# A message path folded into the next weight matrix: root spread by four transposes, squares on ScalarE, and work passed between VectorE and GpSimd

## The chip, the cores and the metric

The kernel runs on one core of one Trainium2 chip. The metric is the device time of one execution in microseconds (us); the time of before is the median of three runs. TensorE is PE in the rows, VectorE is DVE, ScalarE is ACT, GpSimd is POOL, SyncE is SP.

## What is computed

One layer for a graph of 12,500 nodes with 256 channels: a graph part on gathered rows, a linear-attention mixer, and a mixture of four experts. Cut to what matters:

```python
xn = layernorm(x)
# graph part: one gathered row of dst per node, four heads of 64, weights from a softmax over heads
tmp = einsum('nh,nhd->nd', alpha[:n], xt[col[:n]])         # xt = xn @ weight
# mixer
Q, K = elu(xn @ Wq) + 1, elu(xn @ Wk) + 1
KV = einsum('nshd,nshv->nhdv', K, v)                        # one matrix per head, summed over all nodes
msg = (Q KV / (Q . sum K)) @ Wm
msg = layernorm(msg, g1, b1)
h   = relu(concat([xn, msg]) @ W1) @ W2
x1  = x + tmp (four times side by side) + xn + layernorm(h, g2, b2)
# experts, on layernorm(x1)
out = x1 + shared_mlp + the two best of four experts, weighted by a softmax of their gates
```

## The kernel before

Nodes are taken in 25 groups of 512 (four tiles of 128 rows; the last group has two tiles of 106 rows). Every product but a few small ones is done as three fp32r products: each operand is split into a high part, rounded to fp32r, and a low part, what is left (`split_mm`, L272 to L274). So each activation needs a `_hi` copy (ScalarE) and a `_lo` subtraction (VectorE or GpSimd) before TensorE can take it.

**Phase 1** (`phase1`, to about 250 us) runs over the groups and sums K, v and the tables of the graph part. In its last three groups `small_constants` and `second_parts` prepare the weights on VectorE, among them the high and low parts of W1, whose message half (rows 256 to 511) is scaled by `g1`.

**The seam** (`turn0`, `turn1` and the turn of `second=True`, 250 to 341 us) ends the sums, makes `kvT` and `G` (`g_hi`, `g_lo`: the per-head matrices times Wm), and fills the pipeline of the second phase.

**Phase 2** (`phase2(i, par)`) is a loop of turns, i = 3 to 24, then `last_turn` and `end_turn`. Three groups are in flight: group i (a: query, denominators, message), group i-1 (b: the hidden layer W1, W2, the residual `base`, the graph part `gnn`) and group i-2 (c: shared MLP, experts, gates, output). Every engine runs its own fixed program, written out by hand in the order of the code, and waits on semaphores (`wait_ge`) that others count up. Nothing reorders it.

The message path, which the change touches, goes so: `p2_m` makes rows of the message in PSUM (banks 6 and 7); VectorE takes mean and variance of each row (`bn_m`, `mv_m`); GpSimd makes `rs_m` = 1/sqrt(variance + eps) and `nm_m` (`rstd`); ScalarE writes the normalised rows `row_n` (`message_rows`); at the start of the next turn TensorE turns them (`transposes(row_n, ...)`, eight of 128x128) into PSUM banks 0 and 1; ScalarE and VectorE split that into `mT_hi` and `mT_lo`; TensorE multiplies them with the message half of W1 (`w1_part(1, ...)`), after 12 products of `w1_part(0, ...)` and 12 of `p2_q` that stand between.

The z path of the same turn goes: `row_z` (ScalarE), eight transposes, `z_hi` (ScalarE), `z_lo` (VectorE, L1507 in the loop), then the products of the shared MLP, the gates and the experts. `feature_low` (L1335) and `feature_high` (L1341) stand with an exponential between them (ScalarE, L983) for the query. `soft_chain_in` (L1373 to L1386), `compare` and `top_weights` make the gate rows (L1437). GpSimd does `h_lo` (twice a turn), `s1_lo` (shown as `s_lo`, L1841), the sum of `base` and `gnn` (L1865) and eight gathers by indirect DMA.

## Time and profile before

| | |
|---|---|
| time, median of three runs | 1325.66 us (1324.2 to 1329.84) |
| the profiled execution | 1322.97 us |
| its span, first to last instruction | 1321.1 us |
| TensorE busy | 1292.3 us |
| VectorE busy | 1105.4 us |
| ScalarE busy | 733.8 us |
| GpSimd busy | 770.7 us |
| mean granted TensorE clock | 0.997 of full |

The profiled execution is one of its own beside the three timed ones; its span leaves out what lies before the first and behind the last instruction. Busy time is the union of the instructions of an engine. The ends of matmuls are modelled, so two of them overlap in the rows, and the distance from start to start says what one costs.

### The profile page before, as it was taken

What the parts mean: (1) busy time and instruction counts of PE and PEld (TensorE: products, weight loads), DVE (VectorE), ACT (ScalarE), POOL (GpSimd) and SP (SyncE); (2) the same over time, 40 slices, a digit from 0 to 9 for tenths busy, and PEclk for the clock granted to TensorE, in tenths of its full rate; (3) what the DMA queues carried; (4) which work ended last, traced back from release to release, by engine and by line L of the source; (5) the groups of instructions that cost most, each with busy time, mean ns of one, the idle gap of its engine ahead of it and who ended that gap; (6) DMA issues with size and microseconds to landing.
All of it is one profiled execution on the core that took longest, in us unless ns stands there. A gap on an engine that the chain in (4) does not pass through costs nothing.

```text
span 1321.1 us, 26301 instructions
## 1 busy us (share of the span) xinstructions
PE 1292.3 (98%) x8812; PEld 1119.4 (85%) x8812; DVE 1105.4 (84%) x2597; ACT 733.8 (56%) x1332; POOL 770.7 (58%) x815
## 2 busy tenths in 40 slices
PE   6999999899999999999999999999999999999998
PEld 5999999876888888888888888888888888888876
DVE  6988777978888888888888888888888888888875
ACT  4555555345645655455645655555645655555654
POOL 5777777745546654655556564655555654655531
PEclk9999999899999999999999999999999999999999
DMA  6787766523212221222111221222111221212000
GB/s 206 245 283 253 251 226 223 165 61 73 65 42 60 77 75 29 76 60 80 50 54 56 80 73 32 76 60 80 44 60 56 80 72 32 76 60 71 26 17 23
DMA packets 65459, 123.23 MB, mean 93 GB/s; under 512 B 31725, under 2 KB 36176, under 8 KB 65422
## 3 DMA queue, kind: packets, MB, share of 16 engines
q1 hardware_dynamic: 57422, 109.25, 25.6%
q0 software_dynamic: 8000, 13.53, 4.8%
q8 instruction: 19, 0.31, 0.1%
q14 instruction: 18, 0.15, 0.0%
HBM read 70.41 MB, written 52.32 MB: 93 GB/s over the span
## 4 chain that ended last, share of the span: by engine, by line
PE 88%; DVE 4%; issue 3%; POOL 2%; DVEq 1%; POOLq 1%; ACT 1%; ACTq 0%
PE psum L272 26%; PE psum L273 25%; PE psum L274 25%; PE psum L484 5%; PE psum L676 3%; PE psum L729 1%; PE psum L667 1%; PE psum L566 1%; PE psum L739 1%; PE psum L559 1%; POOL h_lo L1841 1%; POOL ag L1837 0%; POOLq L1775 0%; POOL xg L1835 0%; DVE kf L1249 0%
## 5 line engine op out<-in xcount | busy, mean ns | idle before, releaser
L1841 POOL TENSOR_TENSOR h_lo<-relu,h_hi 128x1024 fp32r<-128x1024 f32 (+1 forms) x50 | 119.8, 2397 | 142.1 <-ACT h_hi L998 142.0
L272 PE MATMUL psum<-w_hi,h_hi 128*128 128x256 f32 x588 | 164.4, 280 | 1.6 <-POOL h_lo L1841 1.5
L273 PE MATMUL psum<-w_lo,h_hi 128*128 128x256 f32 x588 | 163.8, 278 | 0.0
L274 PE MATMUL psum<-w_hi,h_lo 128*128 128x256 f32 x588 | 163.7, 278 | 0.0
L1841 POOL TENSOR_TENSOR s_lo<-relu,s_hi 128x512 fp32r<-128x512 f32 (+1 forms) x45 | 82.5, 1834 | 95.8 <-ACT s_hi L1099 94.3
L272 PE MATMUL psum<-z_hi,w_hi 128*128 128x512 f32 (+1 forms) x300 | 121.6, 405 | 2.0 <-DVE z_lo L1611 1.1
L1835 POOL DMA_INDIRECT xg<-table_xt,idx x100 | 99.5, 995 | 34.9 <-issue 31.9
L272 PE MATMUL psum<-xT_hi,w_hi 128*128 128x512 f32 (+1 forms) x300 | 119.4, 398 | 0.1
L997 ACT ACTIVATE relu<-psum,h_bias 128x512 f32<-128x512 f32 (+1 forms) x100 | 67.8, 678 | 88.5 <-PE psum L274 88.4
L273 PE MATMUL psum<-xT_lo,w_hi 128*128 128x512 f32 (+1 forms) x300 | 116.9, 390 | 0.0
L274 PE MATMUL psum<-xT_hi,w_lo 128*128 128x512 f32 (+1 forms) x300 | 116.7, 389 | 0.0
L273 PE MATMUL psum<-z_lo,w_hi 128*128 128x512 f32 (+1 forms) x300 | 116.6, 389 | 0.0
L274 PE MATMUL psum<-z_hi,w_lo 128*128 128x512 f32 (+1 forms) x300 | 116.2, 387 | 0.0
L272 PEld LDWEIGHTS psum<-w_hi,h_hi 128*128 128x128 f32 x588 | 110.4, 188 | 3.5 <-POOL h_lo L1841 1.9
L1837 POOL DMA_INDIRECT ag<-table_al,idx x100 | 95.2, 952 | 30.5 <-issue 30.5
L274 PEld LDWEIGHTS psum<-w_hi,h_lo 128*128 128x128 f32 x588 | 111.4, 190 | 0.0
L273 PEld LDWEIGHTS psum<-w_lo,h_hi 128*128 128x128 f32 x588 | 110.5, 188 | 1.0
L915 ACT ACTIVATE row_n<-psum,nm_m,rs_m 128x256 f32<-128x256 f32 x98 | 47.4, 564 | 111.4 <-POOL nm_m L1778 111.4
L1470 DVE SCALAR_TENSOR_TENSOR base<-xb,rn,b_bc 128x256 f32<-128x256 f32 x98 | 91.7, 975 | 0.2 <-issue 0.2
L1009 ACT ACTIVATE e<-psum,e_bias 128x512 f32<-128x512 f32 (+1 forms) x100 | 67.3, 676 | 37.2 <-PE psum L274 37.1
L272 PE MATMUL psum<-mT_hi,w_hi 128*128 128x512 f32 (+1 forms) x200 | 80.1, 401 | 0.9 <-DVE mT_lo L1619 0.9
L1811 POOL TENSOR_TENSOR k_lo<-kf,k_hi 128x1024 fp32r<-128x1024 f32 x25 | 63.0, 2521 | 30.3 <-DVE k_hi L1253 30.3
(274 smaller groups left out, 4298.1 us busy)
## 6 DMA issues: line engine op xcount, KB each, us to landing
xb<-in_x SPq DMA_DIRECT2D x47, 448.0 KB, 3.5
xT_hi_table<-x1T_hi SPq DMA_DIRECT2D x25, 512.0 KB, 2.8
xT_lo_table<-x1T_lo SPq DMA_DIRECT2D x25, 512.0 KB, 3.6
xT_hi<-xT_hi_table SPq DMA_DIRECT2D x25, 512.0 KB, 3.8
xT_lo<-xT_lo_table SPq DMA_DIRECT2D x25, 512.0 KB, 4.7
table_xt<-xts SPq DMA_DIRECT2D x24, 455.0 KB, 3.0
out<-xmid SPq DMA_DIRECT2D x24, 448.0 KB
xb<-in_x SPq DMA_DIRECT2D x47, 64.0 KB, 3.6
```

Of the source, the lines that this page charges most:

```text
L272: pe.matmul(out, wh, xh, start=first, stop=False)
L273: pe.matmul(out, wh, xl, start=False, stop=False)
L274: return pe.matmul(out, wl, xh, start=False, stop=last)
L484: last = pe.transpose(psum[:, b + c, j * R:(j + 1) * R], src[:, j, c * P:(c + 1) * P], ident[0:R, 0:R])
L915: act.activation(out[:, j, :], src(j), ACT.Identity, bias=nm[which][:, j:j + 1], scale=rs[which][:, j:j + 1]).then_inc(S[done], 1)
L997: act.activation(out[:, 0:t * R], colT(b, t=t), ACT.Relu, bias=bias)
L1009: act.activation(e1[:, e, 0:t * R], colT(bank, t=t), ACT.Relu, bias=e1_bias[:, e:e + 1]).then_inc(S["e1_relu"], 1)
L1470: last = stt(base[:, j, :], xb[par][:, j, :], rn2[par][:, 0, j:j + 1], b2_bc[:], ALU.mult, ALU.add)
L1811: ptt(k_lo[par][:], kf[par][:], k_hi[par][:], ALU.subtract).then_inc(S["k_split"], 1)
L1835: pool.indirect_dma_start(xg[par][:, j, :], None, table_xt.ap(), bass.IndirectOffsetOnAxis(idx[par][:, 1, j:j + 1], 0)).then_inc(S[f"gath{ ...
L1837: pool.indirect_dma_start(ag[par][:, j, :], None, table_al.ap(), bass.IndirectOffsetOnAxis(idx[par][:, 0, j:j + 1], 0)).then_inc(S[f"gath{ ...
L1841: ptt(out, src, hi, ALU.subtract).then_inc(S[done], 1)
```

## The change

- **The message is no longer normalised in rows.** The mean is taken out by centring the rows of Wm (`wm`, in `small_constants`). `G` times diag(g1) times the message half of W1 is multiplied out once, in the seam (`gT`, then four fp32 products of 128x512 on TensorE, split by ScalarE and VectorE into `w_hi` and `w_lo`). What W1 is applied to is then the query over its denominator (`qm`, transposed already), times the root `rs_m` of each node.
- **The root** needs the mean square of the message rows only. `p2_m` stays; `message_squares` on ScalarE replaces `bn_m` on VectorE, `message_rstd` on GpSimd has two small operations instead of four. `spread_deviation` on TensorE spreads the root over the partitions: four transposes whose loaded operand is `rs[:, j:j+1]` read 128 times, into one bank, instead of the eight of `row_n`. `over_deviation` on VectorE multiplies `qm` by it. ScalarE then copies `mT_hi` from `qm`, and VectorE makes `mT_lo` (`message_low`).
- **Between VectorE, ScalarE and GpSimd**: `s1_lo` and the sum of `base` and `gnn` go from GpSimd to VectorE, behind the gate rows. The first of four heads of `gnn` goes to ScalarE (`first_head`). Two residual rows instead of one stand early in VectorE's turn. ScalarE's exponential of the query stands ahead of the first relu pair. GpSimd's gathers for the next group stand right behind the second `h_lo`.

```diff
+            def spread_deviation(i, b, t=T):
+
+                pe.wait_ge(S["rs_m"], i)
+                for j in range(t):
+                    last = pe.transpose(psum[:, b, j * R:(j + 1) * R], rs[LM][:, j:j + 1].broadcast_to([R, P]),
+                                        ident[0:R, 0:R])
+                last.then_inc(S["mt"], 1)
...
+            last.then_inc(S["g_mm"], 1)
+            for c in range(CK):
+                for q in range(CK):
+                    last = pe.matmul(psum[:, 0, c * C + q * P:c * C + (q + 1) * P], wm[:, q, c * P:(c + 1) * P],
+                                     kvT[:, q, :], start=True, stop=True)
+            last.then_inc(S["gt_mm"], 1)
...
-                transposes(row_n, MT2_BANK if second else 0, "mt", "m_norm", T * (i - 1))
+                spread_deviation(i, MT2_BANK if second else 0)
                 w1_part(0, 2, 6, xT_old)
                 w1_part(0, 3, 7, xT_old).then_inc(S["xT_free"], 1)
                 if second:
-                    pe.wait_ge(S["mT"], i)
+                    pe.wait_ge(S["qm"], i)
...
+                p2_den(1, 2)
+                pe.wait_ge(S["gt"], 1)
+                for q in range(CK):
+                    for c in range(CK):
+                        last = pe.matmul(psum[:, q, :], gT[:, c, q * P:(q + 1) * P], wslice(w_raw, "W1", 2 + c),
+                                         start=c == 0, stop=c == CK - 1)
+                    last.then_inc(S["gw_mm"], 1)
+                pe.nop().then_inc(S["p1_pe"], 1)
...
-                p2_den(1, 2)
-                transposes(row_n, 0, "mt", "m_norm", 0)
+                spread_deviation(1, 3)
                 w1_part(0, 2, 6, xT0)
                 w1_part(0, 3, 7, xT0).then_inc(S["xT_free"], 1)
+                pe.wait_ge(S["qm"], 1)
+                p2_expand(1, 2)
+                pe.wait_ge(S["gw_split"], 1)
                 pe.wait_ge(S["mT"], 1)
-                for o in range(2):
-                    w1_part(1, o, 4 + o, mT).then_inc(S["h_mm"], 1)
-                p2_expand(1, 2)
-                for o in range(2, 4):
+                for o in range(4):
                     w1_part(1, o, 4 + o, mT).then_inc(S["h_mm"], 1)
                 pe.wait_ge(S["h_relu"], 2)
...
+            def first_head(v, par):
+
+                act.wait_ge(S["gates"], v - 1)
+                act.wait_ge(S["base"], v)
+                act.wait_ge(S[f"y{par}"], 4 * dma16(v, par))
+                for j in range(T):
+                    last = act.activation(gnn[:, j, :], xg[par][:, j, 0:HEAD_CH], ACT.Identity,
+                                          bias=rn2[par][:, 1, j:j + 1], scale=soft_e[:, 1, j, 0:1])
+                last.then_inc(S["gnn0"], 1)
...
+                if not second:
+                    first_head(i - 1, 1 - par)
+                act.wait_ge(S["qm"], i)
+                act.activation(mT_hi[:], qm[:], ACT.Copy).then_inc(S["mT_hi"], 1)
...
                     z_rows()
+                    p2_exp(i)
                     act.wait_ge(S["e2_lo"], i - 2)
                     first_relu(0)
-                    p2_exp(i)
                     z_high()
...
+            def message_squares(i):
+
+                if due(i):
+                    act.wait_ge(S["rs_m"], i)
                 t = tiles(i)
-                normalize(row_n, lambda j: rowt(6, j, t), LM, "m_norm", t)
+                for pair in range(2):
+                    act.wait_ge(S["m_mm"], 2 * i + pair + 1)
+                    for j in pair_of(pair, t):
+                        last = act.activation(rowt(6, j, t), rowt(6, j, t), ACT.Square,
+                                              scale=1.0 / math.sqrt(C), accum_out=ssq[:, j:j + 1])
+                last.then_inc(S["ssq"], 1)
...
+                dve.reduce_sum(wm_nmean[:], wm[:], AXX)
...
+                for c in range(CK):
+                    ts(wm[:, c, :], wm[:, c, :], wm_nmean[:, c:c + 1], None, ALU.add)
...
-            dve.wait_ge(S["w_hi"], 3)
-            for c in range(CK):
-                stt(wslice(w_lo, "W1", 2 + c), wslice(w_raw, "W1", 2 + c), g1_col[:, c:c + 1],
-                    wslice(w_hi, "W1", 2 + c), ALU.mult, ALU.subtract)
...
+            def over_deviation(i, b, t=T):
+
+                now = slice(0, t * R)
+                dve.wait_ge(S["mt"], i)
+                tt(qm[:, :, now], qm[:, :, now], colT(b, t=t).unsqueeze(1).broadcast_to([P, CK, t * R]),
+                   ALU.mult).then_inc(S["qm"], 1)
+
+            def message_low(i, t=T):
+                now = slice(0, t * R)
+                dve.wait_ge(S["mT_hi"], i)
+                tt(mT_lo[:, :, now], qm[:, :, now], mT_hi[:, :, now], ALU.subtract).then_inc(S["mT"], 1)
+
             def phase2(i, par, a=True, b=True, c=True, more=True, second=False):
-                if b:
+                if b and second:
                     residual(i - 1, 1 - par, (0,))
                 if b and not second:
-                    dve.wait_ge(S["mT_hi"], i)
-                    tt(mT_lo[:], colT(0, 2), mT_hi[:], ALU.subtract).then_inc(S["mT"], 1)
-                if b and not second:
-                    graph_layer(i - 1, 1 - par)
-                if a and not second:
+                    over_deviation(i, 0)
...
+                    residual(i - 1, 1 - par, (0, 1))
+                    message_low(i)
+                    graph_layer(i - 1, 1 - par, (1,))
                     feature_low(i, Q_BANK)
+                    graph_layer(i - 1, 1 - par, (2, 3))
                     feature_high(i, Q_BANK)
...
+                if b and c and not second:
+                    dve.wait_ge(S["s1_relu"], 2 * (i - 1))
+                    tt(s1_lo[:], relu[2][:], s1_hi[:], ALU.subtract).then_inc(S["s1_lo"], 1)
+                    bv = base[:].rearrange("p j (h d) -> p j h d", h=HEADS)
+                    tt(bv, bv, gnn[:].unsqueeze(2).broadcast_to([R, T, HEADS, HEAD_CH]), ALU.add).then_inc(S["base"], 1)
...
-                if a:
-                    if due(i):
-                        dve.wait_ge(S["rs_m"], i)
-                    for pair in range(2):
-                        dve.wait_ge(S["m_mm"], 2 * i + pair + 1)
-                        stats(LM, pair_of(pair, t), lambda j: rowt(6, j, t))
-                    aggregate(LM, "mv_m")
...
+                over_deviation(1, 3)
+                dve.wait_ge(S["gw_hi"], 2)
+                tt(w1_message(w_lo), psum[:, 0:2, :], w1_message(w_hi), ALU.subtract).then_inc(S["gw_split"], 1)
+                message_low(1)
...
+            def message_rstd(count):
+
+                pool.wait_ge(S["ssq"], count)
+                if due(count - 1):
+                    pool.wait_ge(S["mt"], count - 1)
+                ptt(veps[LM][:], ssq[:], eps[:], ALU.add)
+                pool.drain()
+                ptt(rs[LM][:], veps[LM][:], neg_half[:], ALU.pow).then_inc(S["rs_m"], 1)
...
+                        if n == 1 and ahead:
+                            pool.wait_ge(S["gnn"], i)
+                            pool.wait_ge(S[f"idx{1 - par}"], 2 * dma16(i + 1, 1 - par))
                         if due(4 * (i - 1) + 2 * n + 2):
                             pool.wait_ge(S["h_relu"], 4 * (i - 1) + 2 * n + 2)
                         low(h_lo[:, 2 * n:2 * n + 2, :], relu[n][:], h_hi[:, 2 * n:2 * n + 2, :], "h_lo")
...
-                if c and not seam:
-                    if due(2 * (i - 1)):
-                        pool.wait_ge(S["s1_relu"], 2 * (i - 1))
-                    low(s1_lo[:], relu[2][:], s1_hi[:], "s1_lo")
-                if b:
-                    if due(i):
-                        pool.wait_ge(S["t"], i)
-                    if due(i):
-                        pool.wait_ge(S["gnn"], i)
-                    if ahead:
-                        pool.wait_ge(S[f"idx{1 - par}"], 2 * dma16(i + 1, 1 - par))
-                    if not seam:
-                        bv = base[:].rearrange("p j (h d) -> p j h d", h=HEADS)
-                        ptt(bv, bv, gnn[:].unsqueeze(2).broadcast_to([R, T, HEADS, HEAD_CH]),
-                            ALU.add).then_inc(S["base"], 1)
-                    if ahead:
-                        gathers(1 - par, (0, 1))
+                if ahead:
+                    gathers(1 - par, (0, 1))
```

TensorE, the start of a turn (`psum` is the output in all rows; above it the last output products of the turn before). Before:

```order
L273 MATMUL psum<-w_lo,h_hi 128x256
L274 MATMUL psum<-w_hi,h_lo 128x256
L484 MATMUL psum<-ident,row_n 128x128 x8
L272 MATMUL psum<-xT_hi,w_hi 128x512
L273 MATMUL psum<-xT_lo,w_hi 128x512
L274 MATMUL psum<-xT_hi,w_lo 128x512
```

and in the change:

```order
L281 MATMUL psum<-w_lo,h_hi 128x256
L282 MATMUL psum<-w_hi,h_lo 128x256
L503 MATMUL psum<-ident,rs_m 128x128 x4
L280 MATMUL psum<-xT_hi,w_hi 128x512
L281 MATMUL psum<-xT_lo,w_hi 128x512
L282 MATMUL psum<-xT_hi,w_lo 128x512
```

Eight transposes of `row_n` became four of `rs_m`; the products around them are the same.

VectorE, the start of the turn that follows the loop, of the same order as those in it. Before:

```order
L281 COMPARE_AND_BRANCH
L1470 SCALAR_TENSOR_TENSOR base<-xb,rn_0,b_bc 128x256
L1496 TENSOR_TENSOR mT_lo<-psum,mT_hi 128x1024
L1484 TENSOR_SCALAR gnn<-xg,soft_e,rn_0 128x64 x4
L1486 SCALAR_TENSOR_TENSOR gnn<-xg,soft_e,gnn 128x64 x12
L1335 TENSOR_SCALAR qf<-psum 128x1024
L1341 SCALAR_TENSOR_TENSOR qf<-psum,qf 128x1024
```

and in the change:

```order
L289 COMPARE_AND_BRANCH
L1545 TENSOR_TENSOR qm<-qm,psum 128x1024
L1518 SCALAR_TENSOR_TENSOR base<-xb,rn_0,b_bc 128x256 x2
L1551 TENSOR_TENSOR mT_lo<-qm,mT_hi 128x1024
L1536 SCALAR_TENSOR_TENSOR gnn<-xg,soft_e,gnn 128x64 x4
L1387 TENSOR_SCALAR qf<-psum 128x1024
L1536 SCALAR_TENSOR_TENSOR gnn<-xg,soft_e,gnn 128x64 x8
L1393 SCALAR_TENSOR_TENSOR qf<-psum,qf 128x1024
```

The product with the spread (`qm`) and a second residual row stand ahead of `mT_lo`, one head of `gnn` has left, and the other three stand around the low part of the query (`qf`, first row).

VectorE behind the gate rows of a turn in the loop, before and in the change:

```order
L1435 CAST scale_rows<-top_hi 128x4x4 x2
L1437 TENSOR_TENSOR scale_rows<-top_e,top_hi 128x4x4
L1527 REGISTER_ALU
L1211 BN_STATS bn_y<-psum 128x6 x2
L1537 REGISTER_ALU
L1538 TENSOR_TENSOR qf<-qf,psum 128x512
```

```order
L1483 CAST scale_rows<-top_hi 128x4x4 x2
L1485 TENSOR_TENSOR scale_rows<-top_e,top_hi 128x4x4
L1589 TENSOR_TENSOR s_lo<-relu,s_hi 128x1024
L1591 TENSOR_TENSOR base<-base,gnn 128x1024
L1594 ISA
L1260 BN_STATS bn_y<-psum 128x6 x2
L1604 REGISTER_ALU
L1605 TENSOR_TENSOR qm<-qf,psum 128x512
```

`s_lo` and the base sum stand now between the gate rows and the statistics of y.

## Rows read from the trace of the kernel before

**Rows 1.** The page, parts 1 and 2: busy time (share) and instructions; clock in 40 slices.
```profile
PE 1292.3 (98%) x8812; PEld 1119.4 (85%) x8812; DVE 1105.4 (84%) x2597; ACT 733.8 (56%) x1332; POOL 770.7 (58%) x815
...
PEclk9999999899999999999999999999999999999999
```

**Rows 2.** Table of stretches: length; busy of PE, PEld, DVE, ACT, POOL; clock; DMA.
```profile
256.00:262.00 6.00, 6.00 (x34) 4.95 (x31) 4.17 (x12) 0.00 (x0) 4.67 (x5) 0.58 0.33 55
640.00:682.50 42.50, 42.50 (x277) 35.72 (x276) 36.45 (x90) 24.09 (x43) 24.13 (x26) 1.00 0.22 62
```

**Rows 3.** TensorE's waits, 225 to 330 us: total, times, longest.
```profile
PE psum L633 <- DVE kx L1359: 1.8, 1, 1.8
PE psum L272 <- POOL k_lo L1811: 1.4, 1, 1.4
PE psum L559 <- DVE qf L1341: 1.0, 1, 1.0
PE psum L484 <- ACT row_z L915: 0.8, 1, 0.8
```

**Rows 4.** TensorE's waits, 1270 to 1300 us.
```profile
PE psum L272 <- DVE z_lo L1611: 1.1, 1, 1.1
PE psum L272 <- DVE mT_lo L1619: 0.9, 1, 0.9
```

**Rows 5.** TensorE in order of time (start, duration in us), and the tile row_n (ns).
```profile
341.52 1.04 PE L484 MATMUL psum<-ident,row_n 128*128 128x128 f32 x8
342.31 0.48 PE L272 MATMUL psum<-xT_hi,w_hi 128*128 128x512 f32 x1
...
1274.70 0.60 PE L484 MATMUL psum<-ident,row_n 128*128 128x128 f32 x4
1275.06 0.36 PE L272 MATMUL psum<-xT_hi,w_hi 128*128 128x256 f32 x1
...
L484 PE MATMUL psum<-ident,row_n x196: 271/272/330, 272.5 to 1275.0; 128*128 128x128 f32 x196
```

**Rows 6.** The turn that starts at 639.6 us, in order of time: PE, DVE, ACT.
```profile
645.79 0.39 PE L274 MATMUL psum<-xT_hi,w_lo 128*128 128x512 f32 x1
646.02 0.40 PE L272 MATMUL psum<-mT_hi,w_hi 128*128 128x512 f32 x1
...
652.42 0.39 PE L272 MATMUL psum<-z_hi,w_hi 128*128 128x512 f32 x1
...
639.81 1.22 DVE L1590 TENSOR_TENSOR xmid<-xmid,psum 128x1024 f32<-128x1024 f32 x1
...
650.99 1.21 DVE L1507 TENSOR_TENSOR z_lo<-psum,z_hi 128x1024 fp32r<-128x1024 f32 x1
...
648.77 1.05 ACT L983 ACTIVATE qf<-qf 128x1024 f32<-128x1024 f32 x1
649.86 1.03 ACT L1033 ACTIVATE z_hi<-psum 128x1024 fp32r<-128x1024 f32 x1
```

**Rows 7.** The same turn, DVE and POOL: small operations beside large ones.
```profile
658.73 1.84 DVE L1373 TENSOR_TENSOR soft<-ag,xg 128x16 f32<-128x16 f32 x1
...
660.73 2.19 DVE L1381 SCALAR_TENSOR_TENSOR soft<-soft 128x16 f32<-128x16 f32 x1
...
658.13 2.41 POOL L1841 TENSOR_TENSOR s_lo<-relu,s_hi 128x1024 fp32r<-128x1024 f32 x1
```

**Rows 8.** The seam in order of time: DVE and PE.
```profile
252.16 1.41 DVE L1354 SCALAR_TENSOR_TENSOR w_lo<-w_raw,g_col,w_hi 128x512 fp32r<-128x512 f32 x2
...
296.45 1.23 DVE L1735 TENSOR_TENSOR mT_lo<-psum,mT_hi 128x1024 fp32r<-128x1024 f32 x1 [0.72 <-ACT mT_hi L1019]
...
261.63 1.02 PE L647 MATMUL psum<-wm,kvT 128*128 128x256 f32 x4
...
262.72 0.39 PE L273 MATMUL psum<-xT_lo,w_hi 128*128 128x512 f32 x1
...
272.55 1.81 PE L484 MATMUL psum<-ident,row_n 128*128 128x128 f32 x8 [0.86 <-ACT row_n L915]
```

More of the change, by code:

```diff
@@ L795, in last_turn @@
                 pe.wait_ge(S["y"], i - 1)
-                transposes(row_n, 0, "mt", "m_norm", T * (i - 1), t)
+                spread_deviation(i, 0, t)
                 w1_part(0, 2, 6, xT_old, t)
@@ L1687, in query_low @@
                     dve.wait_ge(S["qz_hi"], 2 * i + q + 1)
[L1688 removed]
+                    last = tt(z_lo[:, q, :], qm[:, q, :], z_hi[:, q, :], ALU.subtract)
                 last.then_inc(S["qz"], 1)
[L1691 to L1697 removed]
             def turn0():
```

102 lines of the change are left out of this document (46 added, 56 removed), and 3 rows, old and new, of the table SEMAPHORES.

## The prediction, made before the changed kernel was run

> **What bounds the kernel now.** The busy shares and the clock's slices [rows 1] say where to look: TensorE (PE) is busy for 98% of the span, at full clock nearly everywhere, VectorE (DVE) for 84%, GpSimd (POOL) for 58%. A middle turn of the main loop, cut out as a stretch [rows 2], shows what that means: of 42.50 us TensorE is busy in all 42.50, VectorE in 36.5, GpSimd in 24. The list of waits gives TensorE none between 345 and 1265 us; those it has are single ones, in the seam between the phases [rows 3] and in the last turn [rows 4], and one at the start. So in turns 3 to 24 the time is the length of TensorE's own instruction stream. There a change pays only what it takes out of that stream, and costs only where an operand comes later than TensorE's pace asks. In the seam TensorE waits for others, so there every engine counts.
>
> **The steady turns.** The eight transposes of `row_n` open a turn at 341.52 and the first product behind them starts at 342.31: 0.79 us. The last turn has four of the kind, 1274.70 to 1275.06: 0.36 us [rows 5]. The new `spread_deviation` has four of the same 128x128 form, so a turn loses 0.79 - 0.36 = 0.43 us. The tile's count is 196 [rows 5], which is 24 turns of eight and one of four; two of the 24 lie in the seam: 22 x 0.43 = 9.5 us. New is that the loaded operand is one column read 128 times, which no row shows. From below it costs what the plain one does; from above I let the four cost what the eight do, and the gain is nothing. I take the plain price, since both load 128 columns.
> The Trainium skill, "TensorE: Matmul & The Clock Gate", section "Part 4: PE-mode transpose", puts a transpose at about 275 ns in a kernel's context. A single one here has a duration of 272 ns [rows 5], so there the trace agrees, but they start 0.1 us apart. By the page's figure a turn would lose 4 x 0.275 = 1.1 us, and 22 turns 24 us.
>
> Does a new wait eat the 0.43 us? I laid the changed stream on the turn that starts at 639.6 [rows 6].
> - *Message.* TensorE asks for `mT_lo` at 646.02, now 0.43 earlier, 645.6. VectorE's last sum of the turn before starts at 639.81 and ends at 641.0. Then come the product with the spread (priced 1.22, the duration of that sum, of the same width), ScalarE's (ACT) copy `mT_hi` (1.1, priced like the `z_hi` copy with its semaphore), beside which two residual rows fit, and `mT_lo` (1.2): about 644.5. Margin 1.1 us.
> - *z.* This is the narrow place. `z_hi` starts at 649.86, when the exponential (648.77, 1.05) is done; `z_lo` ends at 652.20, and TensorE takes it at 652.42 by its own pace: margin 0.2. Now the exponential stands ahead of the first relu pair, not behind it, and its input `feature_low` (1.2) can start when the query products end (645.79 + 0.39, less 0.43). So 645.8 + 1.2 + 1.1 for the exponential and 1.2 for the pair give 649.3, about when the transposes of `row_z` end; `z_hi` and `z_lo`, 1.1 and 1.2, end near 651.7, against TensorE's 652.0. Margin 0.3.
> - *Work moved to VectorE.* `s1_lo`, the base sum and the product with the spread are 1.2 us each; the statistics of m and one head of four leave. More is given back: the tiny additions at 658.73 and 660.73 take 1.84 and 2.19 us, and the first ends when GpSimd's `s_lo` (658.13, 2.41) does [rows 7]. With `s_lo` and the base sum gone from GpSimd I expect some 0.2 us for each. The two moved operations stand behind the gate rows, and these come by 3.6 us earlier on that account (less where ScalarE's experts hold up the exponential), so `s1_lo` is there when TensorE asks. TensorE never waited for any of it, so I price it at nothing.
> The Trainium skill, "SBUF — State Buffer", has the cause: a VectorE `tensor_tensor` with both inputs in SBUF and a GpSimd operation that reads SBUF exclude each other for a whole instruction. On the rows of 658 us the trace agrees.
> - *ScalarE.* Four squares replace four normalisations of the same shape and no longer wait for GpSimd; the first head (four of 128x64) goes into its idle time ahead of `mT_hi`. The gathers move up on GpSimd, where they held nobody up. Nothing for either.
>
> **The seam** [rows 3, 8]. Here work is added.
> 1. VectorE centres `wm` three groups ahead of the seam: a reduction of 512 columns, two scalings of 256 and small ones, by the 1.2 us for 1024 columns about 1.2 us. VectorE has no idle time there, and TensorE already waits 1.4 for `k_lo`: +1.2.
> 2. The `w_lo` of W1's message half (252.16, 1.41) goes from in front of the copy `kx`, for which TensorE waits 1.8 us. By the exponential behind it some 0.5 of step 1 is left.
> 3. `gT`: four 128x128 fp32 products, 8 records. The four records of `wm,kvT`, 256 columns each, start at 261.63; the second product behind them starts at 262.72, so they end a pitch of 0.23 before it, 262.49: 0.215 each. 128 columns are 0.107, so +0.9.
> 4. TensorE's waits for `q` (1.0) and `row_n` (0.86) go, since the statistics no longer stand between `feature_low` and `feature_high`; the eight transposes there, fed row by row, took 1.81 against 0.60 for four: -3.1. G times W1, 8 records of 512 columns at 0.43, comes in their place: +3.45. With 0.1 for `z_lo`, turn 1 starts its products 0.5 + 0.9 + 0.1 - 3.1 + 3.45 = +1.9 late.
> 5. Behind the spread VectorE needs the product, `w_lo` out of PSUM and `mT_lo`: 0.2 + 3 x 1.2 = 3.9 us. TensorE is there after 12 products at 0.23 and the expansion, 3.2 us: +0.7. GpSimd's `h_lo` in turn 1 then adds 0.4: +3.0 so far.
> 6. In turn 2, VectorE has one `mT_lo` (296.45, after 0.72 idle) ahead of `xmid`: 1.95 us. Now it has the product, 1.1 waiting for `mT_hi`, and `mT_lo`: 3.6, so +1.65. `row_z` hangs on that chain and TensorE on `row_z`, and so does `h_lo`, by the gathers.
> Seam: +4.65 us. Bounds: slack could swallow most of it (+1.5); or the wait for `row_z`, 0.8 us now and near 3 then, brings the clock down. In the seam behind the gap of 1.8 us the clock is 0.58 of full over 256 to 262 [rows 2], half its full level (1.2 of 2.4 GHz) for most of it: 2.5 us lost (+7).
>
> **The last turn** [rows 4]. Two transposes fewer, -0.2, but TensorE already waits 0.9 for `mT_lo` and 1.1 for `z_lo`, and the half-wide product (0.7) stands ahead of ScalarE's copy and so of `row_z`: +0.5 in all.
>
> **Sum**, against the profiled execution (1322.97 us, span 1321.1): -9.5 + 4.65 + 0.5 = -4.35, 1318.6. That execution was 2.7 us faster than the median of the three runs, 1325.66, which is my base: **1321.3 us**, 0.33% less. Half a per cent, 6.6 us, is about what a measurement of this kernel can tell from no change.
>
> **Rivals.**
> - *The seam costs almost nothing (22%).* For it: step 2 cuts the gap behind which the clock fell, and a clock that stays up gives back 2.5 us and more. Against it: the gap before it, for `k_lo`, grows. 1325.66 - 9.5 + 0.5 + 1.5: 1318.
> - *z comes late (10%), slower than before.* Each 0.1 us by which `z_lo` passes its margin costs 2.2 us in all; at 0.2 beyond it the gain is gone, from 0.5 beyond it the kernel is slower by over 0.5%; at 0.7, 1321.3 + 15.4 = 1337. What could do it is VectorE losing its place early in the turn: `mT_lo` now has both inputs in SBUF and can be held up by GpSimd. Against it: GpSimd only issues gathers then.
> - *The repeated column loads slowly (8%)*, four cost what eight do: 1325.66 + 5.15 = 1331.
> - *The clock falls in turn 2 (7%)*: the forecast and 2.5 us, 1324.
> - *Transposes cost their full duration (3%)*: 24 us out of the turns instead of 9.5, 1307.
> - *The forecast (50%)*, its own range 1318.5 to 1324.
> The range 1315 to 1331 takes in all but z late and the full transposes. Faster by over 0.5% (under 1319.0): 0.33, from the first, the fifth and the lower edge of the forecast. Slower: 0.10, z late. Neither: 0.57.
>
> **What would show it.** Right: turns 0.43 us shorter, no TensorE wait in turns 3 to 24, spreads of 0.36 us; the tiny additions near 0.2; turn 3 starting some 4.6 us later than 341.5; a wait for `row_z` of 2 to 3 us near 308. Wrong: a wait for `z_lo` or `mT_lo` in every turn, spreads of 0.8, or a seam with its clock up.

## The result, and the profile after

The changed kernel takes **1332.7 us** (median of 12 executions, 1329.28 to 1335.35), the kernel before 1325.98 in its 12 (1322.27 to 1330.64). The ratio is 1.0041, with a 95% interval from 1.0026 to 1.0056: 0.4% slower, where I had forecast 0.3% faster. The profiled executions stand further apart, 1334.92 against 1322.97, spans 1333.2 against 1321.1, so the traces have 12.1 us to explain, not 6.7. (That difference has a reason too, below.)

The page of the changed kernel, its busy times and two of its rows by slice; they answer to [rows 1]:

```profile
PE 1299.7 (97%) x8730; PEld 1119.8 (84%) x8730; DVE 1056.3 (79%) x2383; ACT 752.6 (56%) x1520; POOL 646.9 (49%) x721
...
PE   6999999897999999999999999999999999999998
...
PEclk9999999899999999999999999999999999999999
```

VectorE went from 84% to 79% and GpSimd from 58% to 49%, as meant. TensorE has fewer instructions and is busy for longer. Three places show where the time went.

**The turns.** The four spreads of the turn at 648 (timeline of TensorE: start, duration, engine, line, operation, names, shapes, count):

```profile
648.06 0.28 PE L282 MATMUL psum<-w_hi,h_lo 128*128 128x256 f32 x1
648.17 0.60 PE L503 MATMUL psum<-ident,rs_m 128*128 128x128 f32 x4
648.52 0.48 PE L280 MATMUL psum<-xT_hi,w_hi 128*128 128x512 f32 x1
```

From 648.17 to 648.52 are 0.35 us, where eight transposes took 0.79 [rows 5]. So the saving is there. And TensorE still waits for nobody: its list of waits for 352 to 1270 us holds a single one, of 0.2 us, for `mT_lo`. Yet the turn is no shorter. Turn 3 starts at 349.58 and turn 24 at 1245.36:

```profile
349.58 0.60 PE L503 MATMUL psum<-ident,rs_m 128*128 128x128 f32 x4
...
1245.36 0.60 PE L503 MATMUL psum<-ident,rs_m 128*128 128x128 f32 x4
```

That is 42.66 us a turn (895.78 / 21). Before, the same two places are 341.52 and 1235.63: 42.58. Something took 0.5 us a turn, in a stream without waits. A stretch of the products of G and z shows what, first before, then after:

```profile
716.30 0.28 PE L273 MATMUL psum<-g_lo,z_hi 128*128 128x256 f32 x1
716.42 0.28 PE L274 MATMUL psum<-g_hi,z_lo 128*128 128x256 f32 x1
716.53 0.28 PE L272 MATMUL psum<-g_hi,z_hi 128*128 128x256 f32 x1
...
717.21 0.28 PE L272 MATMUL psum<-g_hi,z_hi 128*128 128x256 f32 x1
```

```profile
724.22 0.28 PE L280 MATMUL psum<-g_hi,z_hi 128*128 128x256 f32 x1
724.34 0.28 PE L281 MATMUL psum<-g_lo,z_hi 128*128 128x256 f32 x1
724.46 0.28 PE L282 MATMUL psum<-g_hi,z_lo 128*128 128x256 f32 x1
...
725.28 0.28 PE L280 MATMUL psum<-g_hi,z_hi 128*128 128x256 f32 x1
```

Before, the starts are 0.114 us apart (0.91 / 8), after 0.118 (1.06 / 9), in products that the change did not touch. The duration of a row, 0.28, hides this: only the distance from start to start tells it. Over all turns the same holds for the fp32r products of 256 columns (h with the output weights 115.5 ns before, 117.8 after, the mean distance to the next start) and for most of those of 512 (mT_lo 228.3 and 233.1), while the fp32 transposes of `row_z` keep their 99 ns. In the trace of before both distances occur: a stretch begins at 0.118 or 0.233 and after up to some microseconds turns to 0.113, or to between 0.227 and 0.229. After, it mostly stays with the long one.

**The seam** (waits of TensorE, 225 to 345 us; who waited, for whom, us in total, times, longest; [rows 3] before):

```profile
PE psum L280 <- ACT e L1036: 3.0, 1, 3.0
PE psum L280 <- POOL k_lo L1872: 2.4, 1, 2.4
PE psum L492 <- ACT row_z L942: 2.2, 1, 2.2
PE psum L280 <- POOL h_lo L1902: 1.3, 1, 1.3
PE psum L574 <- DVE kden L1412: 1.2, 1, 1.2
PE psum L648 <- DVE kx L1407: 0.8, 1, 0.8
```

The wait for `row_z` is the one that the prediction has. The 3.0 us for an expert's ReLU (`e`) are new, and in no step of it. Followed back on each engine (timelines of TensorE, ScalarE, VectorE and GpSimd, each engine in order):

```profile
331.90 0.39 PE L280 MATMUL psum<-w_hi,h_hi 128*128 128x256 f32 x1 [3.00 <-ACT e L1036]
...
331.04 0.23 ACT L1042 ACTIVATE soft_e<-soft 128x32 f32<-128x32 f32 x1 [7.23 <-DVE soft L1434]
331.18 0.67 ACT L1036 ACTIVATE e<-psum,e_bias 128x512 f32<-128x512 f32 x1
...
320.75 6.09 DVE L1578 TENSOR_TENSOR s_lo<-relu,s_hi 128x1024 fp32r<-128x1024 f32 x1 [0.56 <-ACT s_hi L1025]
326.77 0.28 DVE L1494 TENSOR_SCALAR psum<-psum 128x128 f32<-128x128 f32 x1
...
321.03 4.72 POOL L1902 TENSOR_TENSOR h_lo<-relu,h_hi 128x1024 fp32r<-128x1024 f32 x2
```

The ReLU stands behind the softmax's exponential on ScalarE's queue, that waits for VectorE's soft chain, and VectorE sat 6.09 us in `s_lo`, a subtraction that takes 1.22 us in later turns. It ends at 326.84, 1.1 us (its own work) after GpSimd's two `h_lo`, 4.72 us together, at 325.75.

**The last turn** (waits from 1270 us on; [rows 4] before):

```profile
PE psum L280 <- DVE mT_lo L1551: 2.1, 1, 2.1
PE psum L802 <- DVE s_lo L1666: 1.2, 1, 1.2
PE psum L492 <- ACT row_z L942: 0.7, 1, 0.7
PE psum L280 <- DVE z_lo L1671: 0.6, 1, 0.6
```

And stretches (from and to, length, busy time of the five engines, granted clock, DMA share, GB/s):

```profile
1289.30:1292.60 3.30, 3.30 (x18) 3.30 (x17) 0.96 (x4) 1.48 (x4) 0.00 (x0) 0.50 0.00 0
1296.00:1312.00 16.00, 14.80 (x89) 10.77 (x84) 8.75 (x37) 9.76 (x21) 4.11 (x7) 1.00 0.01 2
```

The wait for `mT_lo` grew from 0.9 to 2.1 us, and behind it the granted clock is 0.50 over 1289.3 to 1292.6, the lower of its two levels (1.2 GHz). In the trace of before it stays at 1.00 there.

The 12.1 us, place by place: turn 3 starts 8.1 us later (349.58 - 341.52), the 21 turns to turn 24 take 1.7 more, turn 24 takes 0.2 less (38.91 against 39.07), and from the last turn's transposes to the end it is 48.9 against 46.4, 2.5 more.

### The profile page after: what moved, and what is told of

It is laid out like the page before. It is cut to its first block, busy times and chain, and to the rows that moved or that the text cites. A ratio compares the mean times of both kernels' runs of the same rounds, so it can differ in the third digit from the quotient of the medians.

```text
span 1333.2 us, 25928 instructions
## 1 busy us (share of the span) xinstructions
PE 1299.7 (97%) x8730; PEld 1119.8 (84%) x8730; DVE 1056.3 (79%) x2383; ACT 752.6 (56%) x1520; POOL 646.9 (49%) x721
## 4 chain that ended last, share of the span: by engine, by line
PE 89%; DVE 5%; ACT 2%; issue 2%; DVEq 1%; POOL 1%; POOLq 1%; ACTq 0%
PE psum L280 26%; PE psum L281 25%; PE psum L282 25%; PE psum L696 3%; PE psum L492 3%; PE psum L749 1%; PE psum L687 1%; PE psum L574 1%; PE psum L581 1%; PE psum L759 1%; PE psum L503 1%; DVE s_lo L1578 0%; DVE mT_lo L1551 0%; POOLq L1827 0%; ACT relu L1024 0%
## 5 line engine op out<-in xcount | busy, mean ns | idle before, releaser
L1902 POOL TENSOR_TENSOR h_lo<-relu,h_hi 128x1024 fp32r<-128x1024 f32 (+1 forms) x50 | 124.0, 2481 | 173.7 <-ACT h_hi L1025 173.7
L1902 POOL TENSOR_TENSOR s_lo<-relu,s_hi 128x512 fp32r<-128x512 f32 x23 | 29.8, 1295 | 209.3 <-ACT s_hi L1138 209.3
L1058 ACT ACTIVATE mT_hi<-qm 128x1024 fp32r<-128x1024 f32 x23 | 24.4, 1060 | 170.8 <-DVE qm L1545 170.8
L1898 POOL DMA_INDIRECT ag<-table_al,idx x100 | 98.1, 981 | 30.5 <-issue 30.5
L1030 ACT ACTIVATE scaleT<-psum 32x128 fp32r<-32x128 f32 x98 | 26.3, 269 | 112.4 <-PE psum L740 111.5
L282 PE MATMUL psum<-mT_hi,w_lo 128*128 128x512 f32 (+1 forms) x200 | 78.4, 392 | 0.0
```

What stands on the lines that cost most here:

```text
L282: return pe.matmul(out, wl, xh, start=False, stop=last)
L1030: last = act.activation(scaleT[0:QUAD, j * R:(j + 1) * R], psum[j * QUAD:(j + 1) * QUAD, 5, 0:R], ACT.Copy)
L1058: act.activation(mT_hi[:], qm[:], ACT.Copy).then_inc(S["mT_hi"], 1)
L1898: pool.indirect_dma_start(ag[par][:, j, :], None, table_al.ap(), bass.IndirectOffsetOnAxis(idx[par][:, 0, j:j + 1], 0)).then_inc(S[f"gath{ ...
L1902: ptt(out, src, hi, ALU.subtract).then_inc(S[done], 1)
```

## The experiments

All turns below are the distance from turn 3's transposes to turn 24's, by 21, from the rows of each trace. Each ratio is against executions of the kernel before on the same chip; e1_layout to e4_eight shared one, e5_before_seam to e8_best a second, e9_from_h to e11_best_256 a third, and e12_xT_192 had a fourth. The kernel before has 1327.96 us on the first and 1325.48 on the second, so medians of different groups are not compared to the microsecond.

**What makes the products slow?** No wait, no instruction of theirs changed. What did change for them: the new tile `ssq`, 16 bytes a partition, stands ahead of most of the tiles. With the filling that the allocator adds, the tiles from `qm` to `e1` stand 64 bytes further than before, those from `s2_hi` on 128. The weights stand ahead of it and did not move. The kernel's helper `sb` has a placement rule of its own: it counts addresses in lines of 64 bytes and puts the tiles marked `HELD` (h, z, the scales, s2) on odd lines and those marked `MOVING` (w and g) on even ones, with a filler where one is needed. At `s2_hi` this filler makes 128 bytes of the 64. The changed kernel keeps the rule; it settles addresses modulo 128 bytes only.

*e1_layout.*

```diff
-        ssq = sb("ssq", [R, T])
...
+        ssq = nmean[LM]
...
-        wm_nmean = sb("wm_nmean", [P, CK], stack=ctx1)
...
         kvT = sb("kvT", [P, CK, P], stack=ctx1)
+        wm_nmean = sb("wm_nmean", [P, CK], stack=ctx1)
```

> The changed kernel, but the new small tile ssq takes the place of the message's mean column, which the change left unused, and the new wm_nmean lies behind the last tile of the first phase: every tile of the turns is then at the address that it has in the kernel before. In the changed kernel all tiles from the rows' tile on lie 64 or 128 bytes further, and its fp32r products stand 118 and 233 ns apart where those of before are partly 113 and 227. Theory A (the places of the tiles make the products slow): the pitch returns to that of before, the turn becomes 42.58 - 0.43 = 42.15 us instead of 42.66, and the time 1332.7 - 21 x 0.5 = 1322. Theory B (what the other engines do at that moment, or the phase in which PE enters a stretch, sets the pitch): the turn stays at 42.6 to 42.7 us and the time at 1331 to 1334.

1321.53 us, 0.9956 of before (0.9938 to 0.9975): faster than the kernel before. Its turns:

```profile
349.46 0.60 PE L503 MATMUL psum<-ident,rs_m 128*128 128x128 f32 x4
...
718.79 0.28 PE L280 MATMUL psum<-g_hi,z_hi 128*128 128x256 f32 x1
718.91 0.28 PE L281 MATMUL psum<-g_lo,z_hi 128*128 128x256 f32 x1
719.02 0.28 PE L282 MATMUL psum<-g_hi,z_lo 128*128 128x256 f32 x1
...
1233.33 0.60 PE L503 MATMUL psum<-ident,rs_m 128*128 128x128 f32 x4
```

42.09 us, 0.49 less than before and 0.57 less than the changed kernel, with the same instructions in the same order; products 0.114 us apart again. Theory A holds. Turn 3 starts as late as in the changed kernel: the seam is another matter.

*e2_pad.* The kernel before, with one line more:

```diff
+        spare = sb("spare", [R, T])
         LX, LM, LY, LZ = (0, 4), 1, 2, 3
```

> The kernel before with one unused tile of 16 bytes a partition where the change has its ssq, and nothing else: all later tiles move by 64 or 128 bytes as in the changed kernel. Theory A (places): the turn grows from 42.58 to about 43.1 us and the time from 1326 to about 1336. Theory B (activity or phase): 42.58 us and 1326, within 0.3%.

1338.06 us, 1.0079 of before (1.0062 to 1.0096); turn 43.10 (347.80 to 1252.93). An unused tile of 16 bytes costs 10 us on the medians (1338.06 - 1327.96), and 11.0 us in the 21 turns of the traces. It also brought a surprise: `s_lo` in turn 2 takes 6.09 us here as well, and TensorE waits 3.0 for the same ReLU, though the seam is that of the kernel before.

*e6_early* and *e7_late* part the tiles that moved. The kernel has an unused tile, `pad`, between `s2_hi` and `kden`.

```diff
(e6_early, on the changed kernel)
-        pad = sb("pad", [P, P])
+        pad = sb("pad", [P, P - 32])
(e7_late, on e1_layout)
-        pad = sb("pad", [P, P])
+        pad = sb("pad", [P, P + 32])
```

> The changed kernel with the unused tile pad 128 bytes shorter: the tiles from qm to e1 stay 64 bytes further than in before (so on the other side of a 128-byte line pair), and all tiles from kden on are back at the addresses of before. Theory A1 (the early tiles' places slow the products down: xT of even turns, qf, row_z, base, xmid, e1): the turn stays at 42.65 us. Theory A2 (the late tiles' 128 bytes do it: xT of odd turns, h, z, s1, mT, the ReLU tiles): the turn falls to 42.1 us, as in e1_layout, and the time to 1321 to 1323.

> The counterpart: e1_layout, with the unused tile pad 128 bytes longer, so that the tiles up to e1 stand as in the kernel before and all from kden on 128 bytes further, as in the changed kernel. Theory A1 (early tiles): the turn stays at 42.1 us. Theory A2 (late tiles): 42.65 us, the time 1332 to 1334. Both may add up (42.3 to 42.4 in each of the two).

e6_early: turn 42.17 (344.49 to 1230.07), 1323.35 us, 0.9991 of before (0.9972 to 1.001). e7_late: 42.68 (345.71 to 1241.96), 1331.72 us, 1.0069 (1.0048 to 1.0089). It is the late tiles; the early ones are worth 0.1 us at most. (The turns of two kernels with the same tiles in the same places differ by up to 0.04 us: 42.58 and 42.62 in the kernel before and e5_before_seam, 42.09 and 42.12 in e1_layout and e8_best.)

*e9_from_h* and *e10_from_relu* part the late ones.

```diff
(e9_from_h, on e1_layout)
+        spare = sb("spare", [P, 32])
         h_hi = sb("h_hi", [P, 4, GR], F32R, side=HELD)
(e10_from_relu, on e1_layout)
+        spare = sb("spare", [P, 32])
         relu = [sb(f"relu{n}", [P, 2, GR]) for n in range(3)]
```

> e1_layout with an unused tile of 128 bytes ahead of h_hi: h, z, s1, the scales, mT, the ReLU tiles and zf stand 128 bytes further (as in the changed kernel), while kden, the gathered rows, xT of odd turns and all earlier tiles stand as in the kernel before. e7_late has shown that the late tiles together make the turn 42.68 us instead of 42.09. Theory A (the operands that TensorE holds or streams next to the weights, from h on, do it): turn 42.6 to 42.7. Theory B (kden, the gathered rows or xT of odd turns do it): 42.1.

> e1_layout with the unused 128 bytes ahead of relu0 instead: no operand of the fp32r products moves against before, only the ReLU tiles, zf and the small tiles that VectorE, ScalarE and GpSimd read and write. Theory A (TensorE's own two operand streams): turn 42.1 us. Theory B (the other engines' tiles): 42.6 to 42.7.

e9_from_h: turn 42.60 (349.87 to 1244.42), one execution of 1333.14 us. e10_from_relu: 42.04 (346.58 to 1229.40), one of 1318.65. So it is among the tiles that TensorE itself reads, h, z, s1 and mT with the scales and s2's low part; the tiles of the other engines behind them don't matter.

*e11_best_256* and *e12_xT_192* ask what about the address counts. Both are built on e8_best, below (1316.19 us, turn 42.12). In e12_xT_192 the three unused tiles stand in for the longer `pad`: from `kden` on its tiles are where e11_best_256 has them, but for xT.

```diff
(e11_best_256)
-        pad = sb("pad", [P, P])
+        pad = sb("pad", [P, P + 64])
(e12_xT_192)
+        sb("spare0", [P, 48])
         xT_hi0 = sb("xT_hi0", [P, CK, GR], F32R)
         xT_lo0 = sb("xT_lo0", [P, CK, GR], F32R)
+        sb("spare1", [P, 16])
         qf = sb("qf", [P, CK, GR])
...
+        sb("spare2", [P, 16])
         xT_hi = [xT_hi0, sb("xT_hi1", [P, CK, GR], F32R)]
```

> e8_best with the unused tile pad 256 bytes longer, so that all tiles from kden on stand 256 bytes further than in before. Theory A (places count modulo 256 bytes): the turn stays at 42.1 us and the time at 1316, where 128 bytes gave 42.7. Theory B (any other distance is as bad, or the place acts in larger steps): 42.6 us or more, 1328; a turn below 41.9 would say that a better place than that of before exists.

> e11_best_256, with xT's four tiles moved to the place that h, z, mT and s1 have in the fast kernels: their address modulo 256 is then 64 more than that of the weights' tiles (it was the same as the weights', or 128 off). Theory A (what counts is the distance modulo 256 between the tile that is held and the tile that streams, +64 the good one): the products with xT stand 228 ns apart instead of 231, 36 of them a turn, so the turn falls by 0.1 us to 41.93 and the time by 2 to 1314. Theory B (xT's place doesn't matter, or only that of h, z and mT): 42.03 us and 1316. If +64 is good only by chance of the present timing, the products with xT get slower, 233 ns and a turn of 42.1.

e11_best_256: turn 42.03 (346.19 to 1228.83), 1315.99 us, 0.9936 of before (0.9917 to 0.9954). 256 bytes change nothing where 128 cost 0.6 us. e12_xT_192: turn 41.97 (344.85 to 1226.31), 1313.45 us, 0.991 (0.9891 to 0.9928). Theory A forecast 228 ns for the products with xT, 41.93 and 1314. Measured are 228.9 for xT_lo (231.1 in e11_best_256), 234.3 for xT_hi with w_hi (237.3), and 231.7 for xT_hi with w_lo (230.8), which got slower. Together that is the 0.06 us by which the turn is shorter, little more than two equal kernels differ by. Of the 2.5 us between the two profiled spans (1314.2 and 1311.7) 1.3 lie ahead of turn 3, where the theory forecast nothing, and the two ratios overlap. So e12_xT_192 fits theory A and does not show it.

The whole of it by the programs' addresses, modulo 256 bytes (w and g, the weights' tiles, stand at 128 in all):

```
                 h z s1 mT   relu   xT even, odd   transposes   turn
before              192       192     0, 128            8        42.58
e2_pad               64        64    64,   0            8        43.10
changed kernel       64        64    64,   0            4        42.66
e7_late              64        64     0,   0            4        42.68
e9_from_h            64        64     0, 128            4        42.60
e6_early            192       192    64, 128            4        42.17
e1_layout           192       192     0, 128            4        42.09
e10_from_relu       192        64     0, 128            4        42.04
e11_best_256        192       192     0, 128            4        42.03
e12_xT_192          192       192   192, 192            4        41.97
```

With the data's tiles 64 bytes past the weights' modulo 256 the turn is 42.0 to 42.2, with them 64 bytes short of it 42.6 to 42.7 (kernels with four transposes; those with eight are 0.45 longer). Which of the two is held and which streams does not matter: G streams past a held z, and z streams past held weights, and both change. All of these kernels keep the helper's rule of odd and even lines; it does not tell the two places apart. Not separated: since w and g never moved, the data's own address modulo 256 bytes may be what counts, and not its distance from theirs.

**Are the transposes worth what I said?** *e4_eight.*

```diff
-                for j in range(t):
+                for j in 2 * list(range(t)):
                     last = pe.transpose(psum[:, b, j * R:(j + 1) * R], rs[LM][:, j:j + 1].broadcast_to([R, P]),
```

> The changed kernel with each spread issued twice, so that TensorE has eight transposes in front of the products of a turn again (the same rows written twice). Theory A (four spreads are worth 0.43 us a turn, and something else ate the saving): the turn becomes 42.66 + 0.43 = 43.09 us, the time 1332.7 + 22 x 0.43 = 1342. Theory B (the transposes were hidden anyway, so that their number doesn't matter): 42.66 us and 1333. If the pitch of the products depends on how PE enters the stretch behind the transposes, the turn may also come out near 42.6 by a return of the pitch of before; the rows of the products would show that.

Turn 43.11 (351.48 to 1256.80), 1343.2 us, 1.0111 of before (1.009 to 1.0132). Four transposes are worth 0.45 us a turn, at the long distance of the products, which did not come back. Theory B falls.

**What made the 3.0 us?** *e3_seam* on the changed kernel, and *e5_before_seam* the same on the kernel before:

```diff
                     tt(bv, bv, gnn[:]...).then_inc(S["base"], 1)
-                    dve.wait_ge(S["s1_relu"], 2 * (i - 1))
-                    tt(s1_lo[:], relu[2][:], s1_hi[:], ALU.subtract).then_inc(S["s1_lo"], 1)
                 if a:
                     one_over_den(i, Q_BANK)
...
                     top_weights(i)
-                if b and c and not second:
+                if b and c:
                     dve.wait_ge(S["s1_relu"], 2 * (i - 1))
                     tt(s1_lo[:], relu[2][:], s1_hi[:], ALU.subtract).then_inc(S["s1_lo"], 1)
+                if b and c and not second:
```

> The changed kernel, but in turn 2 VectorE takes s1's low part behind the gate rows, as in all later turns, and not ahead of the division and the soft chain. In the changed kernel it ran 6.09 us there (1.22 elsewhere) while GpSimd's two h_lo ran, and TensorE then waited 3.0 us for the expert's ReLU that stands behind the soft chain on ScalarE. Theory A (the two engines shut each other out of the operands in SBUF, and this made the 3.0 us): the wait goes, s_lo takes 1.2 us, turn 3 starts 3 us earlier, at about 346.6, and the time falls by 3 to about 1329.7. Theory B (the expert's ReLU was late for another reason, as the later start of turn 2's z rows): the wait stays at 2 us or more, and the time within 1 us.

> The kernel before, but in turn 2 VectorE takes s1's low part behind the gate rows. In the profiled execution of before this subtraction took 2.85 us at 316.1, in that of e2_pad, with the same order of work, 6.09 us, and TensorE then waited 3.0 us for the expert's ReLU. Theory A (in the kernel before the two engines meet there as well, and some of its executions have the long form): the times lie closer together than the 1322 to 1330 of before, and their median falls from 1326 to 1322 or 1323. Theory B (the spread of the times has another source): the median stays at 1326 and the spread too.

e3_seam: VectorE's timeline, TensorE's waits in the seam, and a stretch behind the wait for `row_z`:

```profile
329.69 1.22 DVE L1587 TENSOR_TENSOR s_lo<-relu,s_hi 128x1024 fp32r<-128x1024 f32 x1
```

```profile
PE psum L280 <- POOL k_lo L1871: 2.4, 1, 2.4
PE psum L492 <- ACT row_z L942: 2.2, 1, 2.2
PE psum L574 <- DVE kden L1412: 1.3, 1, 1.3
```

```profile
311.40:314.80 3.40, 3.40 (x16) 2.35 (x20) 3.29 (x7) 2.69 (x4) 2.49 (x4) 0.50 0.44 64
```

The subtraction takes 1.22 us, the wait for the ReLU is gone, turn 3 starts at 345.75, 3.8 us earlier, and the profiled execution took 1331.48 against 1334.92. The median fell less, to 1331.47 (1.0029 of before, 1.0016 to 1.0041), where 1329.7 was expected. The single times suggest why: those of the changed kernel form two groups, six from 1329.3 to 1331.2 and six from 1334.2 to 1335.4; those of e3_seam lie from 1329.7 to 1331.8. By this the long form comes in some executions only. In the traces of e7_late and e6_early, which have the changed kernel's seam, `s_lo` took 2.88 and 2.95 us:

```profile
319.95 2.88 DVE L1578 TENSOR_TENSOR s_lo<-relu,s_hi 128x1024 fp32r<-128x1024 f32 x1 [0.45 <-ACT s_hi L1025]
...
319.03 6.04 POOL L1902 TENSOR_TENSOR h_lo<-relu,h_hi 128x1024 fp32r<-128x1024 f32 x2
```

Here VectorE gets in between GpSimd's two operations, and GpSimd's pair takes 6.04 us instead of 4.72. Who goes first differs between traces with the same order of work. That it also changes from one execution of a kernel to the next is read from the two groups of times; no kernel was traced in both forms.

e5_before_seam: 1320.85 us, 0.997 of before (0.9957 to 0.9983), a little under the 1322 to 1323 expected. All 11 times lie within 1319.2 to 1322.0. The kernel before had 1319.6 to 1328.8 in the runs beside it, again in two groups: twelve up to 1324.7, with a mean granted clock of 0.997 or more, and fourteen from 1325.4, with 0.996 or less. In e2_pad, which has the seam of before and the long form, TensorE's wait for the late ReLU ends at 327.50, and from about its end on the clock is at half (a stretch around it and behind):

```profile
326.50:333.30 6.80, 5.80 (x26) 5.80 (x27) 3.41 (x18) 1.08 (x4) 0.52 (x1) 0.50 0.09 21
```

So the kernel before most likely has both forms too, and its profiled execution was one of the short form (2.85 us); no trace of it shows the long one. That would be why the two profiles stand 12 us apart and the medians 6.7. The form is not all that e5_before_seam changes: its turn 3 starts at 339.49, 2.0 us ahead of the short form of before, and its clock is at half for 3.4 us near 256, where before has 6.8.

**All together.** *e8_best* is e1_layout and e3_seam, and in the last turn:

```diff
+                over_deviation(i, 0, t)
                 residual(i - 1, 1 - par, (0,))
-                over_deviation(i, 0, t)
+                message_low(i, t)
+                add_output(i - 1, 1 - par)
                 residual(i - 1, 1 - par, (1,))
-                message_low(i, t)
```

where `add_output` is the sum `xmid + psum` that ended the turn before it.

> e1_layout and e3_seam together, and in the last turn VectorE divides the message (qm) first and adds the output of the turn before it behind the message's low part, not ahead of both. If the parts add: 1321.5 of e1_layout, less 1.5 for the seam (what e3_seam gave on the median), less 1.5 to 3 for the last turn, where TensorE waited 2.1 us for mT_lo and its clock was then at half for 3.4 us: 1317 to 1319, 0.6% under the kernel before. If the wait in the last turn only moves to the z rows, 1320.

1316.19 us, 0.9939 of before (0.9915 to 0.9963), 1 us under the 1317 to 1319 expected. TensorE waits 0.7 us for `mT_lo` in the last turn, its clock stays at 1.00 there, and the stretch from the last transposes to the end is 46.7 us (its waits from 1255 us on, and that stretch):

```profile
PE psum L280 <- DVE z_lo L1673: 1.2, 1, 1.2
PE psum L280 <- DVE mT_lo L1551: 0.7, 1, 0.7
```

```profile
1267.70:1314.40 46.70, 38.49 (x268) 31.04 (x266) 27.88 (x87) 26.50 (x59) 8.80 (x14) 1.00 0.09 28
```

With xT moved as well (e12_xT_192) it is 1313.45 us, 0.9% under the kernel before.

## Why the prediction was wrong

It said 1321.3 and -4.35 us on the spans; measured are 1332.7 and +12.1.

- **The steady turns, -9.5: the saving was right, the turn was not.** Four transposes are worth 0.45 us (e4_eight) and 0.49 (e1_layout against before, in which the products of h are a little faster too, 114.6 against 115.6 ns), where I had 0.43, and a column read 128 times loads like a plain tile. What failed is the step before it, "the time is the length of TensorE's own instruction stream": I took the distance between the other products as given. It is not a property of the instruction alone, and the new tile ahead of their operands raised it. Price: 42.66 - 42.09 = 0.57 us a turn, 11.9 us in 21 turns. None of my rivals has it. I had read which tiles the diff adds, and costed `ssq` at nothing.
- **Message and z paths.** Right: no wait in the turns but one of 0.2 us. The rival "z comes late" did not happen.
- **Work moved to VectorE, and the tiny additions.** Right on time in the turns: `s_lo` and the base sum take 1.22 us each behind the gate rows, and the tiny additions take 0.18 and 0.17 (1.84 and 2.19 in [rows 7]). The exclusion went at these additions. At the residual rows beside GpSimd's `h_lo` it was before and stays, and nobody waits for them: three took 3.47 us (first row, before), two take 3.01 (second row), where one alone takes 0.48.

```profile
652.12 3.47 DVE L1470 SCALAR_TENSOR_TENSOR base<-xb,rn,b_bc 128x256 f32<-128x256 f32 x3
...
660.26 3.01 DVE L1518 SCALAR_TENSOR_TENSOR base<-xb,rn,b_bc 128x256 f32<-128x256 f32 x2
...
666.53 0.18 DVE L1421 TENSOR_TENSOR soft<-ag,xg 128x16 f32<-128x16 f32 x1
...
666.87 0.17 DVE L1429 SCALAR_TENSOR_TENSOR soft<-soft 128x16 f32<-128x16 f32 x1
```

- **The seam, steps 1 to 6.** The total is right to the end of what they cover, in part by luck:

```profile
272.56 3.70 PE L898 MATMUL psum<-w_raw 128*128 128x512 f32 x8
276.10 0.60 PE L503 MATMUL psum<-ident,rs_m 128*128 128x128 f32 x4
276.45 0.48 PE L280 MATMUL psum<-xT_hi,w_hi 128*128 128x512 f32 x1
...
310.56 1.91 PE L492 MATMUL psum<-ident,row_z 128*128 128x128 f32 x8 [2.17 <-ACT row_z L942]
...
314.92 0.50 PE L280 MATMUL psum<-z_hi,w_hi 128*128 128x512 f32 x1 [0.47 <-DVE z_lo L1569]
```

  G times W1 takes 3.54 us (3.45 forecast). Turn 1 starts its products at 276.45, 2.3 after before's 274.11 (1.9 forecast); turn 2 at 298.36, 3.25 after 295.11 (3.0 forecast); the z products at 314.92, 4.65 after 310.27 (4.65 forecast); `row_z` is waited for 2.2 us. Of the parts, step 1 was 0.9 for 1.2, and step 2 had the copy `kx` earlier than it came: the products behind its transposes start 1.7 late, not 0.5, which the later parts made good. One of these is the clock, which stands in no step. Before, it is at half for 6.8 us behind the wait for `kx` (254.2 to 261.0). Here it is at half for 3.4 us behind the longer wait for `k_lo` (244.8 to 248.2) and for 3.4 us behind those for `kx` and `kden`, 0.8 and 1.2 us (258.4 to 261.8). The rival "the seam costs almost nothing" named both sides, and they cancelled.
- **The seam behind 315 us.** Here it failed by leaving out. I followed VectorE's chain to `row_z` and stopped. Turn 2's `s_lo` runs against GpSimd's two `h_lo`; where it comes last, it takes 6.1 us and the ReLU comes 3.0 late. With the short form turn 3 starts at 345.71 (e7_late), 4.2 after before's 341.52, against 4.65 forecast; with the long form at 349.58. The Trainium skill, "SBUF — State Buffer", section "Who interferes with whom", says that a VectorE operation with two inputs in SBUF and a GpSimd operation that reads SBUF hold each other off for a whole instruction, by order of issue. By that rule the two together take 2 x 2.4 + 1.2 = 6.0 us, and the trace agrees on the length: 6.09 from 320.75 on in the one form, 6.04 from 319.03 on in the other. On who goes first it does not, by the recorded starts: `s_lo` at 320.75 is ahead of the pair at 321.03, and came last. I had used the rule for the turns and not for the seam. My rival "the clock falls in turn 2" is no part of the measured loss: in the changed kernel's trace it stayed up behind `row_z`, in those of e3_seam, e6_early and e7_late it was at half for 3.4 us there, and those have the earlier turn 3. (Ahead of 262 us e3_seam and e7_late have one such stretch of 3.4 us where the changed kernel has two, so over the seam it is 6.8 us in all three.)
- **The last turn, +0.5: a size.** Measured +2.5 from the last transposes to the end. The wait for `mT_lo` grew by 1.2, as the step has it, but behind it the clock was at half for 3.4 us. In e4_eight and e9_from_h, where it stayed up, that stretch is 47.8 us, 1.4 more than before, against 48.9. So 1.4 are the waits and 1.1 the clock.

The sum by what was measured: 21 turns x (-0.49 + 0.57) = +1.7; seam +4.2, and +3.9 in the long form; turn 24 -0.2; last turn +2.5: 12.1 us. My total would have been about right for the tiles at their old places (e1_layout, 0.44% under the kernel before, 0.33% forecast), but partly by luck: that kernel's losses in the last turn and in the seam are larger than I had, and so is its saving of 10.2, and its profiled span, of the long form, is 1321.2 against 1321.1.

## What to carry to other kernels

In a kernel whose TensorE never waits, the distance between the starts of equal products is a number to compare, since a row's duration does not show it; when a change adds or removes a tile, even one of 16 bytes, compare the addresses of the operands before and after, and put new tiles behind them or in unused room. A placement rule in the kernel, as the odd and even lines here, is no proof that a shift is harmless. When a shift of the schedule is followed through a seam, follow it past the first wait, and look at each pair of VectorE and GpSimd operations on SBUF that it moves together. Two groups among the times of one kernel are worth a look before anything is compared with its profile.

## What the runs showed of the hardware

- The distance between fp32r products with both operands in SBUF changes with the addresses of the tiles modulo 256 bytes. With the data (h, z, mT) 64 bytes past the weights it settles at 0.113 us for 256 columns and 0.229 for 512. With it 64 bytes short it stays near 0.118 and 0.233: in those six traces no six such products in a row have a mean under 0.117 or 0.232. Over the kernel it is 0.6 us in a turn of 42. The weights' tiles stood at 128 in every run, so whether the distance counts or the data's own address is open.
- The products with xT, at 0 or 128 bytes from the weights, have spells of 0.227 and others of 0.233; at +64 (e12_xT_192) they mostly keep to 0.229. So 64 bytes past is not the best place at every moment.
- It is not a fixed price of an instruction. Also at the good places a stretch begins with the long distance and changes to the short one, with no change in the instructions (in e1_layout the stretch of G and z that starts at 718.10 does so after four products, 0.5 us; others later or not at all); and the products with xT_lo stood 229.1 ns apart in e9_from_h and 231.1 in e10_from_relu, with xT at the same addresses. What sets the moment is open, and so is the cause inside the chip. Distances other than 0, 64, 128 and 192 bytes were not tried.
- Which of two operations that exclude each other goes first does not follow from the order of work or from the recorded starts: with VectorE's `s_lo` recorded 0.3 us ahead of GpSimd's pair it came last (6.09 us), and recorded 0.9 us behind the pair's start it came in between (2.88, e7_late).
